# One layer of attention and mixture of experts: the first residual is stored early, and the last sum is an accumulating store

## The reference, cut to what matters

```
x = x + attention(layernorm(x))      # a recurrent attention: a running maximum and two scans over time
x = x + ffn(layernorm(x))

ffn(z):
    x1  = z + silu(conv(z) @ pw)               # a causal convolution over 3 tokens, then a product
    rw  = softmax over the top 2 of 8 router logits of x1
    moe = (sum over e of rw[e] * silu(x1 @ W[e] + b[e])) @ out_w + out_b
    h   = rmsnorm(x1 + moe) * norm_w
    return h + gelu(h @ down) @ up             # with biases
```

## Time and profile before

| what | value |
|---|---|
| median of 3 runs | 982.94 us (982.54 to 983.36) |
| the profiled execution's own time | 982.2 us |
| its span, first to last instruction | 980.4 us |
| TensorE busy | 886.0 us |
| VectorE busy | 863.2 us |
| ScalarE busy | 720.5 us |
| GpSimd busy | 227.5 us |
| mean granted clock of TensorE | 0.965 of full speed |
| output stores on SP's queue | 16 of 512 KB, 2.9 us to landing |

### The profile page before, as it was taken

The page is one execution under the profiler, slowest core; times in us unless marked ns, Lnnn a source line. Parts: engine busy times, 40 slices in busy tenths (PEclk is TensorE's granted clock), DMA queues, the critical chain, the costliest instruction groups (busy, mean ns, idle before and its releaser), DMA issues. The chain is left out here.

```text
span 980.4 us, 15792 instructions
## 1 busy us (share of the span) xinstructions
PE 886.0 (90%) x4288; PEld 483.6 (49%) x4288; DVE 863.2 (88%) x1577; ACT 720.5 (73%) x1233; POOL 227.5 (23%) x477
## 2 busy tenths in 40 slices
PE   3554999999999999999999999999999999969895
PEld 2232455554555555554555555555555555535543
DVE  4999799999999999999999999999999998957562
ACT  4755688786978788787878788687878788545643
POOL 3485222113130222113130222113131221111000
PEclk9776999999999999999999999999999999979998
DMA  6110010101010010101010010101001000100000
GB/s 210 44 43 1 1 44 1 65 1 66 0 43 21 0 64 0 64 0 64 0 42 22 0 64 0 64 0 64 0 22 42 22 22 1 44 1 22 1 22 21
DMA packets 28772, 29.66 MB, mean 30 GB/s; under 512 B 2090, under 2 KB 28484, under 8 KB 28484
## 3 DMA queue, kind: packets, MB, share of 16 engines
q1 hardware_dynamic: 28740, 29.27, 8.8%
HBM read 20.87 MB, written 8.39 MB: 30 GB/s over the span
## 5 line engine op out<-in xcount | busy, mean ns | idle before, releaser
L1295 DVE SCALAR_TENSOR_TENSOR comb<-ye,rw,comb 128x256 f32<-128x256 f32 x448 | 216.3, 483 | 24.9 <-ACT ye L729 10.5
L729 ACT ACTIVATE ye<-pe 128x512 f32<-128x512 f32 x256 | 151.6, 597 | 105.2 <-PE pe L469 90.9
L469 PE MATMUL pe<-weh,x1l 128*128 128x512 f16 x512 | 194.0, 379 | 0.0
L468 PE MATMUL pe<-wel,x1h 128*128 128x512 f16 x512 | 194.0, 379 | 0.0
L467 PE MATMUL pe<-weh,x1h 128*128 128x512 f16 x512 | 194.0, 379 | 0.0
L409 POOL TENSOR_TENSOR msv<-ms,rms_eps_c 128x2 f32<-128x2 f32 x32 | 14.9, 466 | 398.0 <-ACT sq L749 398.0
L465 PE MATMUL pe<-brow,ones 128*128 128x512 f16 x256 | 97.3, 380 | 9.0 <-ACT ye L729 9.0
L380 POOL TENSOR_TENSOR mo<-st 128x4 f32<-128x4 f32 x32 | 12.1, 377 | 317.4 <-DVE st L1101 179.6
L468 PEld LDWEIGHTS pe<-wel,x1h 128*128 128x128 f16 x512 | 50.0, 98 | 60.5
L469 PEld LDWEIGHTS pe<-weh,x1l 128*128 128x128 f16 x512 | 50.1, 98 | 60.4
L467 PEld LDWEIGHTS pe<-weh,x1h 128*128 128x128 f16 x512 | 50.1, 98 | 50.3
(11 more groups left out here) (154 smaller groups left out, 1986.1 us busy)
## 6 DMA issues: line engine op xcount, KB each, us to landing
xa<-in_x SPq DMA_DIRECT2D x16, 512.0 KB, 3.6
xres<-in_x SPq DMA_DIRECT2D x16, 512.0 KB, 4.4
out_y<-yo SPq DMA_DIRECT2D x16, 512.0 KB, 2.9
ye<-in_w_expert SPq DMA_DIRECT2D x2, 1024.0 KB, 6.8
wa<-in_w_attn SPq DMA_DIRECT2D x1, 1024.0 KB, 7.8
wpw<-in_w_pw SPq DMA_DIRECT2D x1, 256.0 KB, 6.0
wout<-in_w_out SPq DMA_DIRECT2D x1, 256.0 KB, 6.2
wdown<-in_w_down SPq DMA_DIRECT2D x2, 64.0 KB, 4.7
```

The lines of the kernel that those rows point to most:

```text
L468: nc.tensor.matmul(dst, x1h[:, h, tok], wel[:, h, cols], start=False, stop=False)
L469: mm = nc.tensor.matmul(dst, x1l[:, h, tok], weh[:, h, cols], start=False, stop=h == H - 1)
L729: act.activation(ye[:, i % NY, :], pe[:, i % 2, :], ACT.Silu, scale=1.0 / WSCALE).then_inc(ye_ready.sem, 1)
L1295: v.scalar_tensor_tensor(out=comb[:, t, :], in0=src, scalar=rw[:, t, e:e + 1], in1=comb[:, t, :], op0=ALU.mult, op1=ALU.add).then_inc(comb ...
```

## The change

The early residual is stored to the output by SP as soon as both halves of `x2` are there, and `yo` becomes `h` plus the up product alone. GpSimd then issues a DMA that adds `yo` to what lies in the output, after it has waited for the early store of the same sequence (`x2_out`) and for `yo`. The copy `x2t`, the sum `xh` and their semaphores go. The waits that kept the buffers apart change with it: `residual` waits for the early store of the sequence before, `scale_h` for the last sum of the sequence before, since `hh` is now read by it.

```diff
@@ SP
-                if on(g):
-                    sp.wait_ge(y_ready.sem, y_ready.at(g))
-                    sp.dma_start(dram_seq(out_tok, g), yo[:]).then_inc(stored.sem, 16)
+                if on(b):
+                    sp.wait_ge(x2_ready.sem, x2_ready.at(b))
+                    sp.dma_start(dram_seq(out_tok, b), x2[:]).then_inc(x2_out.sem, 16)
...
             schedule(sp, body, {-4: stage_experts, -3: gather_biases})
+            sp.wait_ge(x2_out.sem, x2_out.at(B - 1))
             sp.wait_ge(stored.sem, stored.at(B - 1))
@@ GpSimd
                     rstd(b, st2, mo2, pw2, rstd2, shift2, stats2, moments2, rstd2_ready, xn2_ready)
+                if on(g):
+
+                    pool.wait_ge(x2_out.sem, x2_out.at(g))
+                    pool.wait_ge(y_ready.sem, y_ready.at(g))
+                    pool.dma_start(dram_seq(out_tok, g), yo[:], accum_op=ALU.add).then_inc(stored.sem, 16)
                 if on(f):
                     inverse_rms(f, 0)
@@ ScalarE
-                    act.wait_ge(x2_ready.sem, x2_ready.at(f))
-                    if on(g):
-                        act.wait_ge(xh_ready.sem, xh_ready.at(g))
-                    act.copy(x2t[:], x2[:]).then_inc(x2t_ready.sem, 1)
                     act.preload_act_table_set("silu_and_others")
                     silus(0, (0, 1))
@@ VectorE, residual
-                        dve.wait_ge(x2t_ready.sem, x2t_ready.at(f))
+                        dve.wait_ge(x2_out.sem, x2_out.at(f))
@@ VectorE, last_sum
-                    dve.wait_ge(xh_ready.sem, xh_ready.at(g))
+                    dve.wait_ge(h_ready.sem, h_ready.at(g))
...
-                        v.scalar_tensor_tensor(out=yo[:, t, :], in0=po[:, i], scalar=1.0 / WSCALE, in1=xh[:, t, :],
+                        v.scalar_tensor_tensor(out=yo[:, t, :], in0=po[:, i], scalar=1.0 / WSCALE, in1=hh[:, t, :],
@@ VectorE, scale_h
-                        dve.wait_ge(xh_ready.sem, xh_ready.at(g - 1))
+                        dve.wait_ge(y_ready.sem, y_ready.at(g - 1))
@@ VectorE, body
-                if on(g):
-
-                    dve.wait_ge(h_ready.sem, h_ready.at(g))
-                    dve.wait_ge(x2t_ready.sem, x2t_ready.at(g))
-                    if on(g - 1):
-                        dve.wait_ge(y_ready.sem, y_ready.at(g - 1))
-                    v.tensor_tensor(xh[:], x2t[:], hh[:], ALU.add).then_inc(xh_ready.sem, 1)
```

More of the change, by code:

```diff
@@ L135, in build @@
         x2 = sb("x2", [P, NT, C])
-        x2t = sb("x2t", [P, NT, C])
         st2 = sb("st2", [P, NT, 6])
@@ L170, in build @@
         ht = sb("ht", [P, H, T])
-        xh = sb("xh", [P, NT, C])
         ffg = sb("ffg", [2 * HID, T])
@@ L247, in build @@
         h_ready = sig("h_ready", NT)
-        xh_ready = sig("xh_ready", 1)
-        x2t_ready = sig("x2t_ready", 1)
+        x2_out = sig("x2_out", 16)
         t4_done = sig("t4_done", 2)
```

## The result

| | before | after |
|---|---|---|
| median of 17 runs, same chip, us | 982.82 | 984.72 |
| the profiled execution, us | 982.2 | 985.94 |
| its span, us | 980.4 | 984.2 |
| mean granted clock of TensorE | 0.965 | 0.961 |

The ratio of the times is 1.0027 (95%: 1.0019 to 1.0034): the changed kernel is slower by 2.6 us, 1.9 to 3.3. The means of the runs, 982.34 and 984.98, differ by as much; the medians differ by 1.9 only, because the runs before lie in two groups (980.6 to 981.9 and 982.5 to 983.6) and their median falls into the upper one. One of the 17 executions after took 5201 us and is left out of the ratio and the mean; nothing here explains it.

The account below looks back on a forecast made before the run. TensorE was taken as the bound (busy 886.0 of 980.4 us), its loop waits fixed by `gap`. Profiled 982.2 - 1.2 (last fill) + 3.6 (last store) = 984.6, plus 0.74 to the median: 985.3 us; range 981.0 to 991.

Parts of the forecast that it names:

- The last store: Open end after the last `yo`: accumulating store reads, then writes, +3.6 us; bounds +0 and, with GpSimd preparation, +8.5.
- rival B: Last store: accumulating is little dearer than plain, +0 to +3.2 us, 981.7 to 984.9 us, within the measurement; chance 0.32.
- The last fill: TensorE's 1.31 us wait for `ye`: without the copy 1.06 us earlier, without `xh` 0.1; gain 1.2 us.
- The loop: Steady sequences: TensorE's two waits there are fixed by `gap`, so removing `xh` and `x2t` gains 0.
- Rival D: Loop: freed time does reach TensorE, all 6.6 us of waits for `ye` go, 978.7 us; chance 0.10.
- The cover: First 15 accumulating stores: 16 us until GpSimd's `msv` hide them, against 11.4 us for the dearest store; no cost.
- rival C: GpSimd preparing stores holds VectorE up: 991.9 us if mild, near 1024 if dear; chance 0.10.
- The sum: Whole kernel: profiled 982.2 - 1.2 + 3.6 = 984.6 us; against the runs' median 985.3, or +2.4.
- Rival E: TensorE's clock in the tail: its fall moves elsewhere, up to -1.5 us; 980.2 us with a cheap store; chance 0.04.

Follow-up runs that it names:

- experiment 1: Changed kernel with GpSimd's stores made plain instead of accumulating, so the output lacks the first residual; 981.93 us, ratio 1.0003 to the kernel before.
- experiment 2: Changed kernel, but the last of 16 sequences has its residual summed on chip and `yo` stored plainly by SP; 980.86 us, ratio 0.9986 to the kernel before.
- experiment 6: Kernel before without the last sequence's copy `x2t`, and with SP's last store in two halves; 981.33 us, ratio 0.9984.
- Experiment 4: Kernel before, all stores plain on SP, without the last sequence's copy `x2t` (the last `xh` reads `x2`); 981.63 us, ratio 0.9991.
- Experiment 3: Changed kernel with copy `x2t` and sum `xh` put back in their old places, the sum read by nothing; 986.47 us, ratio 1.0040 to the kernel before.
- experiment 5: Changed kernel with the last sequence summed on chip and stored by SP in two halves, each once ready; 980.28 us, ratio 0.9978 to the kernel before.

## Why the prediction was right, step by step

**The last store: the right place, mis-sized.** The term was +3.6, all of it landing; the end grew by 4.32. The landing grew by 3.1 only (6.0 against 2.9). The rest is an issue 0.79 us behind `yo` instead of 0.02, and an end 0.9 us behind the landing instead of 0.4. By experiment 1 the accumulation makes 2.7 of the 4.32 and the queue 1.6, which the sum took as free: it had a preparation in the upper bound alone. That the 2.7 are a read ahead of the write, the reason given, is not shown: the page counts 20.87 MB read with 16 accumulating stores as without, and in the DMA view the bytes move slowly over four microseconds rather than late and fast. With experiment 2 the loss disappears, so the place is shown. The Trainium skill's fit for this queue (DMA: Bandwidth & Descriptors, Anatomy of one DMA — SWDGE (gpsimd) path) gives an estimate of 3.2 us for 512 KB. The plain store of experiment 1 landed in 3.4, in agreement. For the accumulating one, 5.9 to 6.0, it is short by nearly half, and the measurement decides: rival B fails on the sum, not on the queue.

**The last fill: right.** At the same clock the stretch from the down products to the third expert group fell from 7.32 to 6.12 us (experiment 1): the -1.2 of the sum, with a wait of 0.29 left of the 1.31. Its two parts were off a little, in opposite senses: the copy alone gave 0.95 (experiment 6) and not 1.06, since the table load now starts 0.63 us after `ffh` does, where the copy had started 0.52 after it. That leaves 0.25 for the sum `xh`, not 0.1. Experiment 4, the copy alone, measured -0.9. Experiment 3 takes the fill and the loop's gain (below) back, 1.8 by both, and measured 1.3. In the profiled pair it can't be seen in the stage, since the low clock on the down products took 1.70 us back (3.68 us now; before, four of them at the full clock took 1.98).

**The loop: nearly right.** The 0.23 us did move into the 0.37 us, as one wait of 0.70, because ScalarE still waits for `gap`. VectorE's longer idle before `lg` was 0.61 us, not "about 1". But the term 0 was mis-sized: the loop is shorter by 0.64 us over 11 sequences. Rival D, which wanted 6.6, has the right sign at a tenth of its size. The rows show its way: the distance from `lg` to `gap`, which the prediction took as fixed, is 6.42 us instead of 6.50, and 0.07 of this is the first scan behind `lg`. VectorE and GpSimd there before, and VectorE after:

```profile
553.82 1.29 DVE L1018 TENSOR_TENSOR_SCAN aa<-fd,ev 128x512 f32<-128x512 f32 x1
553.83 0.20 POOL L386 TENSOR_TENSOR mo<-mo,ln_eps_c 128x4 f32<-128x4 f32 x1
...
553.68 1.22 DVE L1017 TENSOR_TENSOR_SCAN aa<-fd,ev 128x512 f32<-128x512 f32 x1
```

The scan took 1.28 to 1.29 us in 10 of 12 sequences between 160 and 820 us before and in experiment 6, in two of experiment 3, in one of experiment 4, and in none of the kernels without the copies and sums. Ten times 0.07 is 0.7 of the 0.79 us between the two profiled executions. With `xh` gone, GpSimd's steps start 1.1 us ahead of `lg` instead of 0.5, so they no longer fall into the start of the scan. That it is GpSimd's step that lengthens the scan is suggested by the rows and not tested, and for experiments 3 and 4 this leaves some tenths open.

**The cover and rival C: right.** The 16 us held. The expert sums `comb` take 483 ns on the mean over 448 in both kernels, and `num` beside the store's instruction 1.22 us, its usual length. The store's instruction took 1.32 us in the loop beside VectorE and 1.35 us at the end, with VectorE idle, so neither held the other up. The Trainium skill (SBUF — State Buffer, Who interferes with whom) has a rule that VectorE's two-port modes starve this preparation. No run here tests it: no row shows that `comb` or `num` beside the store use such a mode.

**The sum.** The terms as measured, against what each kernel took:

| kernel | terms, us | their sum | measured |
|---|---|---|---|
| the change | end +4.3, fill -1.2, loop -0.6 | +2.5 | +2.6 (+1.9 to +3.3) |
| 1 plain stores | end +1.6, fill -1.2, loop -0.6 | -0.2 | +0.3 (-0.6 to +1.2) |
| 2 last on chip | end +0.1, fill -1.2, loop -0.6 | -1.7 | -1.4 (-2.2 to -0.5) |
| 3 work put back | end +4.5 | +4.5 | +3.9 (+2.7 to +5.1) |
| 4 one copy gone | fill -1.0 | -1.0 | -0.9 (-1.7 to 0.0) |
| 5 and halves | end -0.7, fill -1.2, loop -0.6 | -2.5 | -2.2 (-3.0 to -1.3) |
| 6 before, halves | end -0.5, fill -1.0 | -1.5 | -1.6 (-2.5 to -0.7) |

The end is each kernel's own. The fill is that of experiment 1, or of experiment 6 where only the copy is gone. The loop is the difference of the two groups, and TensorE's clock is left out. Every sum lies in its interval, but the intervals are 1.4 us wide and more, so they bear out the sums and not each small term. That the forecast of +2.4 came out so near is partly luck, since two errors cancel: the end was taken 0.7 too low, the loop 0.6 too high.

**Rival E.** The clock in the tail didn't turn in the change's favour: it was 0.50 from 967 to 972, and the last four down products took 3.78 us (3.46 before). In experiment 1 the mean of the same stretch was 0.67; from 926 to 928 it was 1.00 there, against 0.50 in the change, and the row 13 to 14 took 41.69 us instead of 43.10. So shifts of about 1.5 us occur among kernels that are alike up to there, and no single profile tells them from an edit.

## What to carry to other kernels

Ask of a store which of its copies stands on an open end: 15 accumulating stores cost nothing that could be told here, and the sixteenth cost 4.3 us and with it the whole change. Sum the last piece on the chip and store it plainly, and split that store so that the first half leaves while the second is summed; the version that does so (experiment 5) is 2.2 us faster than before. Work that is taken from an engine counts where nothing else sets the end of its wait: one copy of sixteen was worth about 1 us, the copies and sums of eleven sequences in the loop some 0.6 us together.

## What the runs showed of the hardware

- The accumulating store moves 512 KB at up to 201 GB/s, the plain one from either queue at 328 to 360 in its full slices. It goes out in 528 packets, the plain store from the same queue in 144, while SP's plain store has 528 as well and is as fast as the other plain one: this speaks for the sum and against the number of packets as what slows the transfer. A plain store of 528 packets from GpSimd's queue was not run. GpSimd's instruction may follow that number; it took 0.65, 0.80, 0.93 and 1.35 us for 48, 144 (plain), 144 (accumulating) and 528 packets, so not alone.
- The early store of `x2`, a plain one from SP, lands in 5.9 us, 3.0 later than the store of the same size from the same queue had taken. It stands behind `xa` and `xres`; no wait in the trace names it.
